# One kernel for four chained layers: in the first stage's loop, head norm and copy of places moved forward, the masks of three banks laid before the keys are copied, and row sums ahead of a transpose

## What is computed

```
x = x + wkv(w, u, k=layernorm(x), v=ctx)              # decayed running sums over the 128 tokens
x = x + attention(layernorm(x), Wa, Wp, w_std, w_rec) # 16 heads of 32, causal softmax, y @ Wp
x = x + mlstm(q=layernorm(x), k=ctx, v=ctx, Wi, bi, Wf, bf, ln_scale)
#   D = exp(log_D - max), C = (q k / sqrt(32)) * D, divided by max(|sum C|, exp(-max)),
#   h = C v, normalised per head, times ln_scale
x = x + experts(layernorm(x)) # softmax(x @ gate_w), top 8 of 32, slots up to a capacity,
#   silu(x w_gate) * (x w_up) @ w_down, weighted and added back per token
```

```
scores = einsum('bhtd,bhsd->bhts', Qf, Kf) * scale
scores = where(causal, scores, finfo.min)
attn = softmax(scores, axis=-1)
out = einsum('bhts,bhsd->bhtd', attn, V)
```

```
probs = softmax(x @ gate_w); w, sel = top_k(probs, 8)
pos = arange(P) - start[se]            # running count of tokens that chose the expert
slot = where(pos < C, se * C + pos, E * C)
```

## Time and profile before

| | us |
|---|---|
| median of 3 runs | 2291.1 |
| runs | 2279.65 to 2293.32 |
| the profiled execution's own time | 2280.3 |
| its span | 2278.4 |

### The profile page before, as it was taken

One profiled execution on the slowest core, in us unless ns is written; L12 is line 12 of the kernel. 1 busy time (PEld: TensorE's weight loads), 2 busy tenths in 40 slices (PEclk: granted clock), 3 DMA queues, 4 the chain that ended last, 5 costly groups with the idle time before them and its releaser, 6 DMA issues. The chain is left out here.

```text
span 2278.4 us, 66453 instructions
## 1 busy us (share of the span) xinstructions
PE 1981.2 (87%) x22199; PEld 1451.0 (64%) x22232; DVE 1572.0 (69%) x3221; ACT 1202.9 (53%) x3018; POOL 1543.7 (68%) x1663
## 2 busy tenths in 40 slices
PE   2898999899989989998438999899999999998996
PEld 2676666666666666666326776676776777776664
DVE  6678877787787777776325675676666667766664
ACT  3566666665655665665224554555454455544542
POOL 4247777676676767776677676777766777777774
PEclk9999999999999999999669999999999999999999
DMA  3111101110100110101028787777877877887875
GB/s 118 44 39 35 32 28 37 32 32 28 37 28 28 37 32 28 32 32 36 24 59 176 160 178 146 159 164 164 174 176 152 174 169 170 166 177 143 173 144 85
DMA packets 136028, 219.44 MB, mean 96 GB/s; under 512 B 28032, under 2 KB 61184, under 8 KB 135936
## 3 DMA queue, kind: packets, MB, share of 16 engines
q0 software_dynamic: 73472, 139.82, 31.9%
q1 hardware_dynamic: 57856, 70.17, 9.8%
q10 hardware_dynamic: 4608, 8.39, 1.0%
HBM read 133.07 MB, written 96.73 MB: 101 GB/s over the span
## 5 line engine op out<-in xcount | busy, mean ns | idle before, releaser
L2087 POOL DMA_INDIRECT out_dram<-y,m_add x300 | 497.4, 1658 | 222.3 <-POOLq L2095 159.5
L2237 PE MATMUL ps<-xh,wh 128*128 128x256 f16 (+1 forms) x1752 | 381.6, 268 | 4.4 <-PEq L2249 2.2
L2238 PE MATMUL ps<-xh,wl 128*128 128x256 f16 (+1 forms) x1752 | 381.5, 267 | 0.0
L555 POOL DMA_INDIRECT slot_scratch<-pair,slots x256 | 301.7, 1179 | 70.3 <-issue 58.2
L2079 POOL DMA_INDIRECT xg<-z_scratch,slot_t x260 | 263.5, 1014 | 84.6 <-issue 76.2
L2318 ACT ACTIVATE y<-ps,wts_now 128x512 f32<-128x512 f32 x294 | 185.4, 682 | 150.5 <-ACTq L2317 129.9
L2242 PE MATMUL ps<-xl,wh 128*128 128x256 f16 (+1 forms) x1752 | 228.6, 267 | 2.7 <-PEq L2253 2.3
L2392 DVE SCALAR_TENSOR_TENSOR hx<-ps,s 64x256 f16<-64x256 f32 x146 | 62.3, 426 | 239.3 <-issue 142.0
L2237 PEld LDWEIGHTS ps<-xh,wh 128*128 128x128 f16 x1752 | 171.8, 98 | 52.5 <-issue 24.2
L2334 ACT ACTIVATE xh<-ps 128x512 f16<-128x512 f32 x146 | 87.2, 597 | 218.5 <-ACTq L2333 185.7
L2238 PEld LDWEIGHTS ps<-xh,wl 128*128 128x128 f16 x1752 | 171.9, 98 | 28.9 <-issue 0.5
(11 more groups left out here) (318 smaller groups left out, 5111.0 us busy)
## 6 DMA issues: line engine op xcount, KB each, us to landing
wst<-in_L_ffn_w_gate_dram SPq DMA_DIRECT2D x32, 384.0 KB
wst<-in_L_ffn_w_up_dram SPq DMA_DIRECT2D x32, 384.0 KB
xt<-in_x_dram SPq DMA_DIRECT2D x32, 256.0 KB
ct<-in_ctx_dram SPq DMA_DIRECT2D x32, 256.0 KB, 2.6
out_dram<-x SPq DMA_DIRECT2D x32, 256.0 KB, 2.0
z_scratch<-zn ACTq DMA_DIRECT2D x32, 256.0 KB
wdst<-in_L_ffn_w_down_dram SPq DMA_DIRECT2D x32, 256.0 KB
out_dram<-y,m_add POOLq DMA_INDIRECT x300
```

What stands on the lines that cost most here:

```text
L555: pool.indirect_dma_start(out=slot_d[:, :], out_offset=bass.IndirectOffsetOnAxis(ap=slots[:, k:k + 1], axis=0), in_=pair[:, k, :], in_offs ...
L2087: pool.indirect_dma_start(out=acc_d[:, :], out_offset=bass.IndirectOffsetOnAxis(ap=m_add[:, k, h:h + 1], axis=0), in_=y[:, k, h, :], in_of ...
L2237: pe.matmul(ps[:, dst, 0:cols], wh[:, j, k, c0:c0 + P], xh[:, k, 0:cols], start=(k == 0), stop=False)
L2238: pe.matmul(ps[:, dst, 0:cols], wl[:, j, k, c0:c0 + P], xh[:, k, 0:cols], start=False, stop=False)
```

## The change

- TensorE: the 16 masks of the scores are laid by a new function `score_masks`. Those of banks 0, 1 and 3 are issued after the wait for the query copy (`q_copy_ready`, new) and before that for the key copy; those of bank 2 after it. The wait for `head_norm` stands ahead of both.
- ScalarE: the two instructions of the head variance stand ahead of `q_copy`, which now signals.
- VectorE: `head_norm` stands ahead of `mark_best` and `weighted_ctx`. `take_places` is only the copy and stands directly behind `row_max`, ahead of `denominator_error`. The addition to the counter is a function of its own, `count_chosen`, behind `wkv_ratio`, with a wait for it ahead of the next `choose`.
- The signal of the places goes from VectorE to TensorE, which passes it on to GpSimd ahead of `v`; before, VectorE signalled GpSimd itself.
- TensorE: `row_sums` stands ahead of the wait for the wkv ratio and `y_turn`; before it stood behind.

```diff
@@ scalar @@
-                    if on(1):
-                        act.wait_ge(q_ps, 1)
-                        act.sem_inc(q_ps, -1)
-                        q_copy()
                     if on(3):
                         act.wait_ge(head_var_ready, 1)
...
                         head_rstd().then_inc(head_rstd_ready, 1)
+                    if on(1):
+                        act.wait_ge(q_ps, 1)
+                        act.sem_inc(q_ps, -1)
+                        q_copy().then_inc(q_copy_ready, 1)
@@ tensor @@
+                def score_masks(banks):
+                    for r in banks:
+                        for q_ in range(4):
+                            i = slice(32 * ((q_ + r) % 4), 32 * ((q_ + r) % 4) + 32)
+                            pe.matmul(ps[32 * q_:32 * q_ + 32, S_BANK + r, :], identb[i, i],
+                                      mask_ts[i, r, :].unsqueeze(1).to_broadcast([32, 4, T]),
+                                      start=True, stop=False, skip_group_check=True)
+
                 def scores():
-                    masks(S_BANK, mask_ts)
...
-                    if on(1):
-                        pe.wait_ge(k_copy_ready, 1)
-                        pe.sem_inc(k_copy_ready, -1)
                     if on(3):
                         pe.wait_ge(head_norm_ready, 1)
                         pe.sem_inc(head_norm_ready, -1)
                         pe.sem_inc(head_norm_ready_for_pool, 1)
                     if on(1):
+                        pe.wait_ge(q_copy_ready, 1)
+                        pe.sem_inc(q_copy_ready, -1)
+                        score_masks((0, 1, 3))
+                        pe.wait_ge(k_copy_ready, 1)
+                        pe.sem_inc(k_copy_ready, -1)
+                        score_masks((K_BANK - S_BANK,))
                         scores().then_inc(scores_ps, 1)
...
                     if on(4):
                         pe.wait_ge(places_taken, 1)
                         pe.sem_inc(places_taken, -1)
+                        pe.sem_inc(take_places_ready, 1)
                     if on(1):
                         v().then_inc(v_ps, 1)
+                    if on(1):
+                        pe.wait_ge(exps1_ready, 1)
+                        pe.sem_inc(exps1_ready, -1)
+                        pe.wait_ge(exps0_ready, 1)
+                        pe.sem_inc(exps0_ready, -1)
+                        row_sums().then_inc(row_sums_ps, 1)
                     if on(0):
                         pe.wait_ge(wkv_ratio_ready, 1)
                         pe.sem_inc(wkv_ratio_ready, -1)
-                    if on(1):
-                        pe.wait_ge(exps1_ready, 1)
-                        pe.sem_inc(exps1_ready, -1)
-                    if on(0):
                         y_turn().then_inc(y_turn_ps, 1)
                     if on(1):
-                        pe.wait_ge(exps0_ready, 1)
-                        pe.sem_inc(exps0_ready, -1)
-                        row_sums().then_inc(row_sums_ps, 1)
                         pe.wait_ge(v_copy_ready, 1)
@@ vector @@
                 def take_places():
-                    dve.tensor_copy(pos[:, :], ps[:, PL_BANK, 0:E]).then_inc(take_places_ready, 1)
+                    return dve.tensor_copy(pos[:, :], ps[:, PL_BANK, 0:E])
+
+                def count_chosen():
                     return dve.tensor_tensor(selacc[:, :], selacc[:, :], selb[:, :], ALU.add)
...
-                    if on(0):
-                        weighted_ctx().then_inc(dve_step, 1)
+                    if on(3):
+                        dve.wait_ge(head_rstd_ready, 1)
+                        dve.sem_inc(head_rstd_ready, -1)
+                        head_norm().then_inc(head_norm_ready, 1)
...
-                    if on(3):
-                        dve.wait_ge(head_rstd_ready, 1)
-                        dve.sem_inc(head_rstd_ready, -1)
-                        head_norm().then_inc(head_norm_ready, 1)
+                    if on(0):
+                        weighted_ctx().then_inc(dve_step, 1)
+                    if on(5):
+                        dve.wait_ge(counted, 1)
+                        dve.sem_inc(counted, -1)
...
                     if at == 1:
                         low_p_weights()
+                    if on(4):
+                        dve.wait_ge(places_ps, 1)
+                        dve.sem_inc(places_ps, -1)
+                        take_places().then_inc(places_taken, 1)
...
                         wkv_ratio().then_inc(wkv_ratio_ready, 1)
+                    if on(4):
+                        count_chosen().then_inc(counted, 1)
```

More of the change, by code:

```diff
@@ L363, in build @@
             places_taken = once("places_taken")
+            counted = once("counted")
+            q_copy_ready = once("q_copy_ready")
             minus_running_max_ready = once("minus_running_max_ready")
@@ L1855, in step @@
                         low_first_rows(0)
[L1856 to L1859, removed]
                     if on(2):
```

## The result

| | before | changed kernel |
|---|---|---|
| median, 6 runs each | 2291.9 us | 2303.1 us |
| runs | 2279.65 to 2296.8 | 2299.93 to 2305.38 |
| ratio, 95% interval | | 1.0057 [1.0042, 1.0072] |
| profiled span | 2278.4 us | 2303.5 us |
| start of the 7th row maximum | 239.8 us | 247.6 us |

The kernel is 0.6% slower: 11 us by the medians. The two profiled executions lie further apart, because that of the kernel before (2280.3 us) was near its fastest run and that of the changed kernel (2305.4) its slowest. Of the 25.1 us between their spans, 7.9 arise before the seventh row maximum, where the steps are still being filled, and 20.9 in the 25 steps after it; the rest of the program gives back some 4.

The account below looks back on a forecast made before the run. The prediction took GpSimd's cycle (keys, sums, three stores, qk passed on, decayed scores, head sums) to set the short step. Keys 18 + 3 us and fewer long steps 8 gave 2291 - 29 = 2262 us, own range 2248 to 2278.

Parts of the forecast that it names:

- in a short step the cycle that sets the period runs through GpSimd: Loop steps of 31.17 us: keys, sums, three stores, qk passed on, decayed scores and head sums set the period.
- 18 + 3 for the keys: GpSimd's keys start 0.7 us earlier: 18 us over 26 loop steps, some 3 in steps outside the loop.
- 8 for long steps: First-stage loop: 3 fewer of the steps that cost 2.8 us more, 8 us gained.
- I charge 0: Row sums delay y's transposes, making first residual, next x's load, third norm and division 0.2 to 0.6 us late: priced 0.
- The cover named: VectorE's 1.61 us wait before the decayed scores was to hide the late residual; without it, 0.6 us a step.
- The load of the next x: Listed among what comes 0.2 to 0.6 us late with the first residual; no separate price.
- Places: Places copy moved forward, signalled through TensorE: GpSimd's keys gain 0.7 us a step, bounds 0 and 0.75.
- about 0.1 after: If TensorE passes the signal early, GpSimd's keys start about 0.1 us after its residual ends, 0.75 us gained.
- Masks: 12 of 16 mask matmuls run in TensorE's key-copy idle: 0.4 us a step, worth nothing alone where GpSimd sets the period.
- Rival C: Slower: log_d ends after GpSimd's second store begins in all steps, so none is short; 2296 to 2314 us, chance 0.13.
- Rival A: All loop steps become short as the third norm falls into and stretches GpSimd's first store; 2220 us, chance 0.25.
- B: Nothing gained: TensorE passes the places late or VectorE's stretch merely moves, keys start as before; 2287 us, chance 0.20.

Follow-up runs that it names:

- before_again: The kernel before, unchanged, traced again in a later comparison: 0.9993 of before, 29.71 us a step.
- after_again: The changed kernel, unaltered, run again in a later comparison: 1.0080 of before, 30.05 us a step.
- sums_stats: Kernel before with only row sums ahead of y's transposes, plus statistics of the next x moved behind the attention output's low part: 1.0075 of before.
- after_direct: Changed kernel, but VectorE takes the places copy's signal and gives it to GpSimd itself, without TensorE: 1.0078 of before.
- after_no_run: Changed kernel without GpSimd's stores of pairs 4, 5 and 6, second stage not comparable: 1.0043 of before, 30.03 us a step.
- places_alone: Kernel before with only the places copy moved forward and signalled through TensorE, counter's addition behind the ratio: 1.0021 of before.
- masks_alone: Kernel before with only head norm and head variance moved forward and masks of banks 0, 1, 3 before the key copy: 0.9941 of before.

## Why the prediction was wrong

**The steps that failed** are two. The first is "in a short step the cycle that sets the period runs through GpSimd": all of the forecast gain, 18 + 3 for the keys and 8 for long steps, 29 us in all, hung on it, and the keys and stores came 1.0 us earlier without one step getting shorter. The second is "I charge 0" for the late transposes of y, which turned the level result into a loss.

**The charge of 0.** The residual was seen to come 0.2 to 0.6 us later, and it does: 9.53 us into the step against 9.13 at the first level, 9.50 against 8.85 at the other (0.4 and 0.7); in the first steps it is 1.15 later at both. The cover named was VectorE's 1.61 us ahead of the decayed scores. That is idle time of VectorE. What the lateness meets is TensorE, whose idle time at that place is 0.16 us. Timelines of VectorE and TensorE, one step each, `before_again` (row maximum at 469.47) and `after_again` (at 479.92):

```profile
480.55 1.14 PE L1296 MATMUL ps<-Rt,Lt 32*128 32x512 f32 x8
...
480.88 0.69 DVE L1720 TENSOR_TENSOR oT<-ps,rinv 128x512 f32<-128x512 f32 x1
...
481.83 1.17 PE L1304 MATMUL ps<-qT,kT 32*128 32x128 f32 x32
```

```profile
489.42 0.69 DVE L1716 TENSOR_TENSOR x1n<-xt,ps 128x512 f32<-128x512 f32 x1 [0.89 <-DVEq L1922]
...
490.93 1.14 PE L1305 MATMUL ps<-Rt,Lt 32*128 32x512 f32 x8
...
492.02 0.68 DVE L1734 TENSOR_TENSOR oT<-ps,rinv 128x512 f32<-128x512 f32 x1
...
492.96 1.17 PE L1313 MATMUL ps<-qT,kT 32*128 32x128 f32 x32 [0.89 <-PEq L1463]
```

Before, the division ends (481.57) while `log_d` still runs (to 481.69), so TensorE shows no idle time. After, it ends at 492.70 and `log_d` at 492.07. The ends alone would leave 0.1 us of slack, but the signal has its own way, through ScalarE: `qk` starts 0.93 to 0.96 us after the division starts in each of 30 steps of all 18 traces, two steps with 1.2 us apart, before the change too (480.88 and 481.83). So the division already set the start of `qk`, it had no slack at all, and the 0.7 us by which it was moved were paid in full there. The text named the division among what would be late and `qk` among what waits, and then took its cover from another engine. Its own price without the cover, 0.6 us a step, is of the right size: the whole diff costs 0.34 us a step at the second level, with 0.45 given back by the masks part.

**The load of the next x** was named too and given no price. In the filling steps it is the main link. Timelines around the projection, `before_again` and then `after_again`:

```profile
93.88 0.33 SPq L471 DMA_DIRECT2D xt<-in_x_dram  x1
...
96.58 0.69 DVE L1569 BATCH_NORM_STATS2 st<-xt 128x6 f32<-128x512 f32 x1 [0.27 <-DVEq L1732]
...
98.33 0.38 PE L1176 MATMUL ps<-wph,oh 128*128 128x512 f16 x1 [0.68 <-PEq L1327]
```

```profile
96.98 0.33 SPq L473 DMA_DIRECT2D xt<-in_x_dram  x1
...
99.61 0.70 DVE L1581 BATCH_NORM_STATS2 st<-xt 128x6 f32<-128x512 f32 x1 [1.26 <-DVEq L1746]
...
101.66 0.38 PE L1178 MATMUL ps<-wph,oh 128*128 128x512 f16 x1 [1.97 <-PEq L1336]
...
103.75 0.63 PE L1178 MATMUL ps<-wph,oh 128*128 128x512 f16 x1
```

The load takes 2.6 to 2.7 us from issue to use in both, and TensorE's gap grows from 0.68 to 1.97 us. Behind it the product of 0.38 us takes 0.63: the granted clock is 1.00 up to the gap and falls to half behind it (0.57 on average from 101.6 to 105.6), and that step is 32.1 us where it was 28.7. The same step at the first level has the same numbers (1.97 us ahead of the projection, 32.1 us long), so there the 7.9 us have this cause. The load alone does not account for all of the first steps: `sums_stats` still has 3.3 us of the 9.2.

**What bounds the kernel** was read wrong. GpSimd's spread of sums came 1.1 us earlier in the changed kernel's steps, and its wait at the start of the next step grew with it, from 33.4 us to 49.4 over the loop. The sign was there before: in the step of the earlier trace rows GpSimd's copy of the context, first in its next turn, already waits 0.88 us behind the third store. `after_direct`, `after_no_run` and `places_alone` say the same at the other level, where all that shortens GpSimd's way gains nothing. What sets the period there is TensorE, with waits of 1.25 us in a step of 29.7.

**Places.** Forecast 0.7 us a step, 18 in the loop; measured alone, the loop is 0.9 us longer. The keys did start 1.0 earlier at the first level (4.68 against 5.65), by way of an earlier residual, but not "about 0.1 after" it: 1.47 after. So the signal that TensorE passes on came late: the keys start 0.65 us after `minus_max` began (725.81) and 0.36 before `v`. And early keys shortened no step. The Trainium skill, TensorE: Matmul & The Clock Gate, gives its queue a depth of 64 in the table at its head. `minus_max` is 32 products, each with a load of its weights, so by that page the pass is reached about when its first product leaves the queue, not when the product before it is issued. The trace agrees roughly: GpSimd's queue takes the signal at 726.30, 0.49 us after the first product began. The prediction drew an early pass from the same figure without counting the products.

**Masks.** Forecast 0.4 us a step, then called worth nothing where GpSimd sets the period. Measured alone 0.45 a step and 0.6% of the time. The size was right, and the discount was the error.

**Rival C** is the case that came: slower, 2296 to 2314 us. Its condition held in every step of the loop: the second store begins before `log_d` ends, in the step shown at 11.4 against 12.7 us (`log_d` takes 2.0 us there and not 1.14). The three steps of the shorter kind have the pause ahead of `qk` too. In the trace before, the same condition parts the steps of the loop without exception: in 17 of them the second store begins 0.27 us ahead of the end of `log_d`, and ScalarE's queue sees `log_d` done 2.7 us after that end; in the 9 others the store begins with the end or just behind it, and ScalarE's queue sees it 0.07 us after. So at the first level the rows speak for C's reading, that signals of TensorE come late while GpSimd issues stores; with the stores 1.1 us earlier the late one is that of `weighted_v`. At the other level the condition held in `masks_alone` and `after_again` without one long step, and the stores could be left out without effect. Which of the two the first comparison's loop obeys was not tested at that level.

**Rival A.** Its condition, that the third norm falls into the first store of the run, did not come about: the norm starts at 11.07 us, when that store, from 9.99, has just ended. The store took 1.1 us and 23 of 26 steps are long.

**The sign.** The forecast and the rivals A and B all rested on the same reading of GpSimd. The right price, from rows then at hand, would have been 0.5 to 0.7 us in each of 26 steps against the masks' 0.4: slower or level.

**What stays open.** Why the kernel, changed or not, ran 7% slower in the first comparison than in all later ones. The four later comparisons ran on four chips and agree to 0.2%; which chip the first ran on is not on record. Its traces show the excess in the first stage as pauses of TensorE ahead of and inside `qk`, marked as issue, with the clock low behind them, and its shorter steps too are 1.5 us longer than those of the other level (0.7 of it a wait ahead of `places`, L1401, which the other level has in one step only). In the second stage a part of it is longer waits at one line. No later run showed these pauses, so no experiment touched them. So it is also open why the change left only 3 shorter steps there, and whether GpSimd's stores have a part in that. Of the first comparison's loss the 7.9 us in the first steps have the cause that the experiments show. The 20.9 us of the loop do not follow from it: of the 1.2 to 1.3 us by which the division is late there, the late residual explains 0.1 and the late signal of `weighted_v` the rest.

The masks part alone beats both kernels: 0.9941 of before, twice, and 1.4% under the changed kernel.

## What to carry to other kernels

When a step of work comes later, follow it to the next instruction of the engine that sets the pace and read the slack there, as the arrival of the signal that it waits for against the end of what it is busy with; idle time of the engine in between is no cover. A distance between the two instructions that is the same in every step (here 0.94 us from division to `qk`) says that there is no slack, even where no idle time shows. Price each thing that hangs on the moved step separately, transfers too: here there were at least two links, and removing one only moved the wait to the other. Effects of parts need not add up: one part was worth nothing alone and something beside another. A wait whose removal the profile invites should be checked for what ends last behind it: in `before_again` the keys' wait for the places would have ended at 3.7 us into the step, and the residual ahead of them ends at 5.2.

## What the runs showed that was not expected

The same program ran at two levels 7% apart, 2280 to 2297 us and 2129 to 2144, with nearly the same durations of instructions; the difference was in pauses and in the clock behind them, so what bounds the kernel was read at one level and tested at the other. On VectorE, the addition that took 2.08 us in the loop took 0.68 in every step of the changed kernel and at the other level, since it no longer met GpSimd's residual, and yet no step got shorter by it; in `after_direct` it meets the residual again, takes 2.2 us, and the step stays at 30.1. Seven stores issued earlier in GpSimd's order cost 2.5 us a step.
